# q and k as fp16 parts, transposed by DMA: a decoder layer on one core

## The reference

```python
q = _apply_rope((x @ w_q.T).reshape(Bt, S, HEADS, HEAD_DIM), sin, cos)
k = _apply_rope((x @ w_k.T).reshape(Bt, S, HEADS, HEAD_DIM), sin, cos)
scores = jnp.einsum('bhqd,bhkd->bhqk', q, k)
attn = softmax(where(causal, scores, -1e9) / 8)
x = layernorm(x + (attn @ v) @ w_out.T)
```

## Time and profile before

| | us |
|---|---|
| median of 3 runs | 1349.67 (1349.12 to 1350.99) |
| the profiled execution, its time | 1352.37 |
| its span, first to last instruction | 1350.6 |
| TensorE busy | 1328.9 (98%) |
| VectorE busy | 1037.7 (77%) |
| ScalarE busy | 648.3 (48%) |
| GpSimd busy | 232.2 (17%) |
| mean granted clock of TensorE | 0.997 of 2.4 GHz |

### The profile page before, as it was taken

One profiled execution on the slowest core, in us unless ns is written; L12 is line 12 of the kernel. 1 busy time (PEld: TensorE's weight loads), 2 busy tenths in 40 slices (PEclk: granted clock), 3 DMA queues, 4 the chain that ended last, 5 costly groups with the idle time before them and its releaser, 6 DMA issues. The chain is left out here.

```text
span 1350.6 us, 22505 instructions
## 1 busy us (share of the span) xinstructions
PE 1328.9 (98%) x7082; PEld 661.3 (49%) x7082; DVE 1037.7 (77%) x1873; ACT 648.3 (48%) x1241; POOL 232.2 (17%) x270
## 2 busy tenths in 40 slices
PE   8999999999999999999999999999999999999998
PEld 3455455555545545545545554444444444444443
DVE  5998456456488688688688677998888888888875
ACT  6888564465455355455455444333333333333321
POOL 0003222122231222221221230210000000000010
PEclk9999999999999999999999998999999999999999
DMA  9615644444434534434434576444444444444412
GB/s 376 249 43 186 216 148 153 168 141 166 170 112 154 179 110 162 170 114 163 165 112 164 165 232 197 108 117 115 107 110 112 107 107 107 109 114 113 113 46 68
DMA packets 127962, 194.75 MB, mean 144 GB/s; under 512 B 79424, under 2 KB 90928, under 8 KB 127920
## 3 DMA queue, kind: packets, MB, share of 16 engines
q1 hardware_dynamic: 127920, 194.22, 46.7%
HBM read 153.02 MB, written 25.43 MB: 132 GB/s over the span
## 5 line engine op out<-in xcount | busy, mean ns | idle before, releaser
L581 PE MATMUL ps<-weights,xT 128*128 128x512 f16 x2112 | 470.8, 379 | 1.8 <-DVE rope_s L1170 0.8
L581 PEld LDWEIGHTS ps<-weights,xT 128*128 128x128 f16 x2112 | 203.8, 98 | 236.9 <-issue 6.9
L836 PE MATMUL ps<-weights 128*128 128x512 fp8e4 (+1 forms) x1536 | 303.9, 358 | 0.2 <-DVE attn L1671 0.2
L836 PEld LDWEIGHTS ps<-weights 128*128 128x128 bf16 x1536 | 145.9, 98 | 155.9 <-issue 5.6
L1120 ACT ACTIVATE attn<-ps,xscale 128x512 f32<-128x512 f32 x96 | 61.4, 639 | 235.0 <-PE ps L836 235.0
L581 PE MATMUL ps<-weights 128*128 128x512 f16 x768 | 168.7, 379 | 0.0
L813 PE MATMUL ps<-weights 128*128 128x512 fp8e4 x672 | 147.8, 379 | 0.0
L867 ACT COPY attn<-ps 128x512 f32<-128x512 f32 x128 | 68.4, 585 | 156.3 <-PE ps L572 156.3
L935 ACT ACTIVATE attn<-attn,negmax,undo 128x128 f32<-128x128 f32 x256 | 122.7, 482 | 7.3 <-DVE negmax L1362 7.2
L581 PEld LDWEIGHTS ps<-weights 128*128 128x128 f16 x768 | 75.0, 98 | 89.6
L813 PEld LDWEIGHTS ps<-weights 128*128 128x128 bf16 x672 | 65.3, 98 | 75.8 <-issue 0.5
(11 more groups left out here) (171 smaller groups left out, 1694.6 us busy)
## 6 DMA issues: line engine op xcount, KB each, us to landing
wch<-w_ffn SPq DMA_DIRECT2D x96, 688.0 KB, 4.3
wch<-sim_scratch SPq DMA_DIRECT2D x96, 128.0 KB
ternary_scratch<-tern SPq DMA_DIRECT2D x48, 172.0 KB, 1.9
ctx<-ctx SPq DMA_DIRECT2D x16, 512.0 KB
wo_raw<-x_scratch SPq DMA_DIRECT2D x16, 512.0 KB, 4.6
x_in<-xT_in SPq DMA_DIRECT2D x15, 512.0 KB, 6.6
weights<-x SPq DMA_DIRECT2D x15, 512.0 KB, 10.4
x_scratch<-weights SPq DMA_DIRECT2D x15, 512.0 KB, 2.9
```

Source lines behind the costliest of these rows:

```text
L581: ins = nc.tensor.matmul(ps[:, bank], partsT[:, a, t], weights[:, t, w, half * HALF:(half + 1) * HALF], start=(t == 0 and a + w == 0), sto ...
L836: ins = nc.tensor.matmul(ps[:, 2 * w + a, 0:n], xqT[:, t], w8m[:, t, at:at + n], start=(t == 0), stop=(t == KT - 1))
```

## The change

From batch 2 on, q and k are kept as two fp16 parts. `rope_add` adds in place, in `rope_c`; `qk_high_part` on ScalarE writes the fp16 high part into `qk_parts` (the memory of q), `qk_low_part` on VectorE the fp16 rest; the next rope waits for the low part, as `rope_c` is in use until then. When q and k of a half are there, SP sends one transposing DMA of 128 x 2048 fp16 values (`load_qkT`) into `qkT16` (the memory of qkT or of k). `scores` multiplies three products of fp16 parts instead of one in fp32, and the transposes `qk_T` and their copies on ScalarE go.

The orders change with it: VectorE takes `mask_max(0)` ahead of rope 0, and `x_maximum`, `x_factors` and `x_undo` earlier; ScalarE's and SP's are in the diff; GpSimd's is rope_add 0, rope_add 1, x_all, rope_add 2, the cosine product, rope_add 3, and in the prelude its all-reduce moves behind rope_add 1. In the last turn VectorE and TensorE start the softmax earlier, and the first half of the output projection is cut in two around `prob_T(0)`. In the second turn (b = 1), q and k of batch 2 get their parts in the same way. Left out below are these two turns, semaphores and some conditions.

```diff
         v = attn[:, 0:D]
         qkT, prob, probT = (attn[:, j * D:(j + 1) * D].rearrange("p (w t n) -> p w t n", w=2, t=4) for j in (1, 2, 3))
+        qk_parts = q[:].bitcast(F16).rearrange("p (m a n) -> p m a n", m=2, a=2)
+        qkT16 = [buf.bitcast(F16).rearrange("p (m a t n) -> p m a t n", m=2, a=2, t=4) for buf in (attn[:, D:2 * D], k[:])]
         negmax = sb("negmax", [P, 2, 4], F32)
         rowsum = sb("rowsum", [P, H], F32)
...
+                sp.wait_ge(qk_low, qk_uses(n, 2 * u + 2))
+                sp.wait_ge(scores_full, n * 2)
+                if isinstance(n, int) and n == 2:
+                    sp.wait_ge(tr_full[1], tr_pair(1, 1) + 1)
+                apart(sp)
+                sp.dma_start_transpose(qkT16[u].rearrange("p m a t n -> p (m a t) n"), qk_parts.rearrange("p m a n -> p (m a n)")) \
+                    .then_inc(qkT_loaded[u], 16)
             def turn(b, mode, has_next, has_next2):
                 def w_load(c):
...
                     sp.dma_start(xres_last, x[b + 1]).then_inc(xres_last_loaded, 16)
...
                     load_w8(0, 4)
...
                     load_sims(1)
                 if mode != "plain":
+                    later = not (isinstance(b, int) and b == 0)
                     for c in range(4 if second else 2, SUMS if mode == "sum" else CUTS):
+                        if later and not second and c == (3 if mode == "sum" else 2):
+                            load_qkT(b + 1, 0)
+                        if later and c == (6 if mode == "sum" and not second else 5):
+                            load_qkT(b + 1, 1)
                         if mode == "cut":
                             w_store(c - 2)
...
                 def scores(u):
+                    if not (isinstance(b, int) and b < 2):
+                        pe.wait_ge(qkT_loaded[u], (b - 1) * 16)
+                        pe.wait_ge(scores_free, b * 4 + 2 * u)
+                        for t in range(4):
+                            for a, w in ((0, 0), (0, 1), (1, 0)):
+                                for r in range(2):
+                                    rows = slice(64 * r, 64 * r + 64)
+                                    ins = nc.tensor.matmul(ps[:, SC + r, t * P:(t + 1) * P], qkT16[u][rows, 0, a, t],
+                                                           qkT16[u][rows, 1, w, t], start=(a + w == 0), stop=(a == 1))
+                        ins.then_inc(scores_full, 1)
+                        return
...
                     return
-                qk_T(0)
+                scores(0)
                 proj(0)
                 if isinstance(b, int) and b == PASS:
                     pe.wait_ge(abs_done, 1)
                     pe.wait_ge(oT_ready, b * 2)
                     nc.tensor.matmul(ps[:, OB, 0:3], ones, abs_sum[:, 0:3], start=True, stop=True).then_inc(abs_summed, 1)
-                scores(0)
-                qk_T(1)
                 proj(1)
                 scores(1)
                 prob_T(0)
...
                 nc.scalar.copy(conv_parts[:, kk, 0], convG[:, kk + 1]).then_inc(conv_high, 1)
+            def qk_high_part(n, j):
+                act.wait_ge(roped, n * 4 + j + 1)
+                if j >= 2:
+                    act.wait_ge(qkT_loaded[0], (n - 1) * 16)
+                elif isinstance(n, int) and n == 2:
+                    act.wait_ge(tr_full[0], tr_pair(1, 1) + 1)
+                else:
...
-                    copy_bank(w, tr_pair(b, 0), qkT[:, w])
-                act.wait_ge(scores_full, b * 2 + 1)
-                for w in range(2):
-                    copy_bank(w, tr_pair(b, 1), qkT[:, w])
                 exps(0)
-                ctx_square()
+                qk_high_part(b + 1, 0)
                 abs_chunk(0)
                 sign_chunk(0)
                 act.wait_ge(pv_full, b * 2)
                 for w in range(2):
                     copy_bank(w, tr_pair(b, 2), probT[:, w])
+                qk_high_part(b + 1, 1)
                 exps(1)
+                oT_high_part(0)
+                ctx_square()
                 abs_chunk(1)
                 sign_chunk(1)
-                oT_high_part(0)
+                qk_high_part(b + 1, 2)
                 abs_chunk(2)
-                abs_chunk(3)
                 act.wait_ge(pv_full, b * 2 + 1)
                 for w in range(2):
                     copy_bank(w, tr_pair(b, 3), probT[:, w])
+                abs_chunk(3)
                 abs_chunk(4)
                 abs_chunk(5)
                 sign_chunk(2)
+                qk_high_part(b + 1, 3)
                 prelude = has_next and not has_next2
                 if prelude:
...
-                dve.wait_ge(roped, n * 4 + (j if at is None else at))
+                if (isinstance(n, int) and n == 1) or (isinstance(n, int) and n == 2 and j == 0):
+                    dve.wait_ge(roped, n * 4 + (j if at is None else at))
+                else:
+                    dve.wait_ge(qk_low, qk_uses(n, j))
                 src = ps[:, OB + j // 2 if raw else PJ + j % 2]
...
+            def qk_low_part(n, j):
+                dve.wait_ge(qk_high, qk_uses(n, j) + 1)
+                nc.vector.tensor_tensor(qk_parts[:, j % 2, 1], rope_c[:], qk_parts[:, j % 2, 0], ALU.subtract).then_inc(qk_low, 1)
...
                     threshold_sums()
+                mask_max(0)
                 rope(b + 1, 0)
-                mask_max(0)
                 if first_cut:
                     thresholds()
                 normalise(0)
                 if prelude:
                     dve.wait_ge(convw_in, 16)
                     nc.vector.tensor_reduce(cfit[:, 0:1], convw, AX_X, ALU.max, apply_absolute_value=True).then_inc(conv_max, 1)
+                qk_low_part(b + 1, 0)
                 rope(b + 1, 1)
                 mask_max(1)
-                ctx_norms()
+                qk_low_part(b + 1, 1)
+                if has_next2:
+                    x_maximum(b + 2)
                 cut_chunk(0)
                 normalise(1)
                 if prelude:
...
                     weigh(0, 0)
                 oT_low_part(0)
+                ctx_norms()
                 if prelude:
                     weigh(0, 1)
                 cut_chunk(1)
+                if has_next2:
+                    x_factors(b + 2)
+                    x_undo(2)
+                qk_low_part(b + 1, 2)
                 rope(b + 1, 3)
                 if prelude:
                     conv_low_part(0, 0)
                     weigh(0, 2)
                     conv_low_part(0, 1)
-                if has_next2:
-                    x_maximum(b + 2)
                 cut_chunk(2)
+                qk_low_part(b + 1, 3)
                 if not prelude:
...
                     return
-                x_factors(b + 2)
                 cut_chunk(3)
                 cut_chunk(4)
-                x_undo(2)
                 low_x(b + 2)
                 dve.wait_ge(xres_loaded, b * 16 + 16)
...
-                pool.wait_ge(tr_full[j % 2], tr_pair(n - 1, j // 2) + 1)
-                nc.gpsimd.tensor_tensor((q, k)[j % 2][:, j // 2 * HALF:(j // 2 + 1) * HALF], rope_c[:], rope_s[:], ALU.add) \
-                    .then_inc(roped, 1)
+                nc.gpsimd.tensor_tensor(rope_c[:], rope_c[:], rope_s[:], ALU.add).then_inc(roped, 1)
             def x_all(n):
...
                         rope_add(b + 1, 0)
+                    rope_add(b + 1, 1)
                     if prelude:
                         pool.wait_ge(conv_max, 1)
                         nc.gpsimd.partition_all_reduce(cfit[:, 1:2], cfit[:, 0:1], P, RMAX).then_inc(conv_max_all, 1)
-                    rope_add(b + 1, 1)
                     if isinstance(b, int) and b == 1:
                         first_rstd(0)
                 second = isinstance(b, int) and b == 1
-                if second:
-                    rope_add(2, 2)
+                if has_next2 and not (isinstance(b, int) and b < 2):
+                    x_all(b + 2)
+                if has_next and not (isinstance(b, int) and b == 0):
+                    rope_add(b + 1, 2)
+                if prelude:
+                    pool.wait_ge(wch_free[1], 3 * WCH)
+                    nc.gpsimd.memset(x1p[:, 0:1], 0.0).then_inc(set_up2, 1)
+                    nc.gpsimd.memset(x1p[:, D + 1:D + 2], 0.0).then_inc(set_up2, 1)
+                    pool.wait_ge(set_up2, 2)
                 pool.wait_ge(ctx_loaded, b * 32 + 32)
                 pool.wait_ge(norms_ready, b + 1)
                 nc.gpsimd.tensor_tensor(sq[:, 0:8], ctx9[:, 0:8], ctx9[:, 1:9], ALU.mult).then_inc(ctx_mult, 1)
                 if not has_next:
                     first_rstd(b)
-                if prelude:
-                    pool.wait_ge(wch_free[1], 3 * WCH)
-                    nc.gpsimd.memset(x1p[:, 0:1], 0.0).then_inc(set_up2, 1)
-                    nc.gpsimd.memset(x1p[:, D + 1:D + 2], 0.0).then_inc(set_up2, 1)
-                    pool.wait_ge(set_up2, 2)
```

(27 more changed lines are left out.)

29 lines of the change are left out of this document (20 added, 9 removed).

## The result

The changed kernel takes **1432.4 us** in the median (1429.7 to 1436.9), against 1349.8 for the kernel before in the same series: a ratio of 1.060, 95% interval 1.059 to 1.062. The profiled execution took 1430.2 us, with a span of 1428.6 against 1350.6.

What follows compares the result with a forecast made beforehand. TensorE, busy without a break, was taken to bound the kernel. 1352.4 + 32.5 (sum turns) + 20.7 (cut turns) + 6 (prelude and last turn) = 1411.6, the runs' median 2.7 lower: 1409 us, range 1378 to 1442.

Steps and rivals of the forecast that it cites:

- Scores: TensorE: each group of 24 fp16 score products takes 0.9 us, between 0.7 and 1.6, in place of 1.1 in fp32.
- The maximum at T+18.0: Looped turn: x's maximum ends 18.0 us after scores(0) starts; GpSimd's next instruction, rope_add 2, follows 13.7 later, at 31.7.
- The cut turn: Eight turns: TensorE waits 3.9 us before the second value product; 52.8 each, 422.4 against 401.7, +20.7.
- the clock's term: Cut turns: work lost to a half clock after the new wait, 0 to 3.4 us a turn, 1.1 taken.
- The sum turn: Four turns: late chunk loads and sums also delay the output projection; 58 us each, 232 against 199.5, +32.5.
- A half clock is hidden here: Sum turns: a half clock adds nothing, since the projection before the output projection then only fills the wait.
- Turn 1: The second batch's turn: forecast to change by 0 us.
- Prelude and last turn: Prelude: TensorE waits of about 2, 2 and 4 us, less 2.2 gained; both turns together +6, between -4 and +12.
- (a): Rival: GpSimd's code swap stays off the path, rope_add 2 done by T+29.3 in a cut turn; 1310 us, chance 0.08.
- (b): Rival: only the swap towards the reduce runs ahead, in loops too; cut turn 48.2, sum turns 54; 1354 us, chance 0.06.
- (c): Rival: the clock stays at half after every wait, in sum turns too; 1445 to 1460 us, chance 0.06.
- (d): Rival: the transposing DMAs are late, deciding at 25 us of landing time; 1420 us and more, chance 0.02.

Runs made afterwards that it cites:

- experiment 1: Changed kernel with only x's all-reduce put back behind rope_add 3 (x_factors and x_undo back too): 1357.0 us, ratio 1.004 to the kernel before.
- experiment 6: Changed kernel with the cosine product moved behind rope_add 3 on GpSimd in the looped turns: 1428.7 us, ratio 1.058 to the kernel before.
- experiment 3: Changed kernel with the two waits before x's all-reduce exchanged, scale first, then maximum: 1412.1 us, ratio 1.045 to the kernel before.
- experiment 8: Changed kernel with turn 1's second v chunk and x's high part ahead of abs_chunk 4, 5: 1425.7 us; three combined versions, reduce behind rope_add 3: 1343.1, 1343.8, 1327.5.

## Why the prediction was right, and where it was off

The direction, the mechanism and the range were right: 1409 forecast, 1432 measured, 1378 to 1442 given. The span came out 78 longer, where 59 was added up. Point by point:

- **Scores.** 0.9 a group taken, 0.8 measured. An unhindered turn was put at 47.5; experiment 1 has 47.26 to 47.69 in its sum turns.
- **The maximum at T+18.0, 13.7 to the next step, rope_add 2 at 31.7, the second value product at 34.8.** Measured 18.1, 13.7, 31.9 and 34.9 in the turn from 608.00. The Trainium skill (GPSIMD Engine Reference, Instruction dispatch) prices the first call of fresh code at some 6 us; the trace agrees with 5.9 on the way in, and the 1389 that 6 on both sides gave is refuted by the 7.1 on the way back in this turn (6.7 to 7.5 in the looped ones).
- **The cut turn.** 52.8 forecast, 54.5 in the mean of the seven looped ones. The step that failed is the clock's term, 1.1: value product and last projection took 1.97 and 6.82 in place of 1.09 and 5.34, which is 2.4. With "rope 3 frees its bank just in time" the cover was too thin as well: low part 2 took 2.10 and not 0.69 (experiment 6), and the last projection waits 0.6. 51.7 + 2.4 + 0.6 = 54.7. By the Trainium skill's rule (TensorE: Matmul & The Clock Gate, HAM oscillation) a loop that waits in each turn has its clock fall each time, and the trace agrees for waits of 3.8 to 4.7: 0.94 over the looped cut turns, though at 2.4 a turn and not 3.4. In turn 6, with waits of 1.3 and 1.6, the clock stays at 1.00.
- **Turn 6** takes 50.4: the swap in ran ahead there, as before, which I took for an exception without asking for its cause (experiment 3).
- **The sum turn.** 58 forecast; 231.8 for the four against 232. In the turn from 277.20 chunk 5 ended at T+43.7 (44 forecast), the second value product started at T+36.4 (36.2), the output projection at T+46.7 (47.3). "A half clock is hidden here" held in the first two turns, where the output projection took 10.53; in the other two it took 12.22 and 11.98. That the four come out at 232 is in part luck: the early start and the half clock nearly cancel.
- **Turn 1.** 0 forecast, 6.6 measured. The step that failed is "on SP they stand ahead of some weight loads, which are not due then": in turn 1 chunk 5's was due, and waited 4.7 behind the DMA. What the runs show is the price of late chunks ahead of the v chunk; how much of their lateness is the DMA's stays open (experiment 8).
- **Prelude and last turn.** +6 forecast, +8.4 measured, within its bounds, but as a difference: the prelude took 10.9 more, the last turn 2.4 less. In the prelude the three waits were put at 2, 2 and 4; they came out at 2.96, 1.43 and 5.77, and the last projection took 7.74 in place of 5.34, a half clock that the sum has no term for.
- **The rivals.** (a) fell: rope_add 2 ended at T+33.1, past 29.3. (b) held for turn 6 alone. (c) held in part: the clock falls in each looped turn, but for 6.9 us in the one shown, and the sum turns are no longer for it than forecast. (d) fell: no product waited for a transposing DMA. But in turn 1 ScalarE waited 3.6 for one, and chunk 5's load stood behind the other, ways that (d) did not name. In (b)'s sum, four turns of 54 are 16.5 more, not 18; it changes nothing here.

Together: turn 1 +6.6, cut turns 431.8 against 422.4, +9.4, prelude and last +2.4: 18 of the 19 us by which the span exceeds the forecast.

## What to carry to other kernels

When a change puts a step ahead of another on one engine's queue, price it by the time from its input to the next step of that queue, not by its own record: here 0.38 us of reduce held GpSimd for 13.7, and 75 of 83 us came back when it moved back by three places. A releaser named in the profile is the last link of a chain; moving that link alone moved the wait to the next product. And a wait that the new order leaves in each turn has a second price, the granted clock behind it, which matmuls put into the wait did not buy off here (1438 us with them, 1432 without), as the engines behind it were as late.

## What the runs showed of the hardware that was not expected

- What GpSimd does around the reduce shows in the trace as pairs of configuration steps, 5.9 us ahead of the reduce and 7.1 ahead of the next step. In the loops the pair ran behind the first of the two waits and ahead of the last: 0.4 us after the maximum's end in the change, 3.3 before it with the waits exchanged (experiment 3).
- A transposing DMA of 128 x 2048 fp16 values lands in 4.4 us in the median, where the 128 x 1024 one takes 3.1, but its issue holds SP's queue for 1.3 to 4.7 us (the landing is that of all 28):

```profile
L454 SPq DMA_TRANSPOSE k<-q x14: 1324/3786/4737, 143.2 to 876.1; - x14
DMA to landing us min/median/max: 4.2/4.4/7.7
```

- A VectorE step on 128 x 512 elements takes 2.1 to 2.8 us beside GpSimd's product of two 128 x 1024 operands, and 0.69 without it; the product takes 2.3 to 3.7. The Trainium skill (SBUF — State Buffer, Who interferes with whom) has a VectorE step with two SBUF inputs contend with a GpSimd step that reads SBUF; the trace agrees, with these numbers, and the forecast left it out.
